# A recommendation tower on one core: packed dot products in two units per tile, eight one-hot features, gathers in two bursts

## The reference

```python
e = jnp.stack([tbl_0[ids[:, 0]], ..., tbl_25[ids[:, 25]]], axis=1)
combined = jnp.concatenate([dense_features[:, None, :], e], axis=1)    # 2048 x 27 x 128
interactions = jnp.einsum('bnd,bmd->bnm', combined, combined)
z = jnp.concatenate([dense_features, interactions[:, _TRIU_I, _TRIU_J]], axis=1)
h = jnp.concatenate([z, dense_features], axis=1)                       # 2048 x 607
h = jnp.maximum(h @ W_top1 + b_top1, 0.0)                              # 512 columns
h = jnp.maximum(h @ W_top2 + b_top2, 0.0)                              # 256 columns
y = h @ W_top3
```

## Time and profile before

| | |
|---|---|
| median of 3 runs | 604.8 us (597.53 to 605.89) |
| profiled execution | 598.93 us, span 597.2 us |
| mean granted clock of TensorE | 0.842 |
| TensorE busy | 466.2 us (78%), 6057 matmuls |
| VectorE, ScalarE, GpSimd busy | 256.7 us (43%), 176.1 us (29%), 296.0 us (50%) |

### The profile page before, as it was taken

How to read it: one execution, slowest core, us unless ns; L and a number is a source line. 1 busy time by engine, 2 the same in 40 slices (tenths; PEclk the granted TensorE clock), 3 DMA queues, 4 the chain that set the end, 5 groups by cost and what they waited for, 6 DMA issues and landing times.

```text
span 597.2 us, 14574 instructions
## 1 busy us (share of the span) xinstructions
PE 466.2 (78%) x6057; PEld 423.9 (71%) x6057; DVE 256.7 (43%) x465; ACT 176.1 (29%) x443; POOL 296.0 (50%) x314
## 2 busy tenths in 40 slices
PE   3564677697988889676997979688797969977787
PEld 1463666586977878576886868677686858877776
DVE  3853458251544446252452626344262623622340
ACT  1231233332324332132322314132232423224341
POOL 7777144554554455455554545555554554545200
PEclk9557689897878988888888979869797796988899
DMA  5453211111111111111111111111111111111000
GB/s 116 157 171 88 73 27 39 38 44 37 36 45 35 42 37 46 38 38 42 36 46 33 46 33 44 38 35 42 41 45 37 33 45 32 41 37 38 23 3 1
DMA packets 19577, 28.02 MB, mean 47 GB/s; under 512 B 10691, under 2 KB 13267, under 8 KB 19518
## 3 DMA queue, kind: packets, MB, share of 16 engines
q0 software_dynamic: 9728, 19.94, 12.7%
q1 hardware_dynamic: 9790, 7.17, 4.1%
HBM read 27.08 MB, written 0.01 MB: 45 GB/s over the span
## 4 chain that ended last, share of the span: by engine, by line
PE 71%; issue 15%; ACT 3%; DMA 3%; another core or an unknown queue 3%; DVE 3%; SPq 1%; DVEq 0%; ACTq 0%
PE dots_ps L394 27%; PE fetch_ps L419 22%; PE h_ps L466 9%; PE vec_ps L372 6%; PE h_ps L482 4%; DMA vecs<-in_tbl 3%; PE ids_ps L401 2%; ACT vecs L607 1%; PE fetch_ps L466 1%; DVE onehot L739 1%; ACT inter L643 1%; DVE inter L818 1%; DVE vecs L590 1%; ACT vecs L590 0%
## 5 line engine op out<-in xcount | busy, mean ns | idle before, releaser
L333 POOL DMA_INDIRECT rows<-in_tbl,idx x304 | 293.5, 965 | 262.5 <-DMA rows<-in_tbl,idx 154.4
L394 PE MATMUL dots_ps<-vecs 128*27 128x27 f32 x4096 | 162.3, 202 | 73.1 <-issue 71.6
L394 PEld LDWEIGHTS dots_ps<-vecs 128*27 128x27 f32 x4096 | 148.1, 118 | 88.4 <-issue 85.8
L419 PE MATMUL fetch_ps<-onehot,t_hi 125*128 125x256 f32 x448 | 136.0, 327 | 38.4 <-ACT vecs L607 24.7
L818 DVE COPY_PREDICATED inter<-mask,dots_ps 27x128 f32<-27x128 int32 (+2 forms) x256 | 66.7, 260 | 205.4 <-ACT inter L643 198.9
L739 DVE TENSOR_TENSOR onehot<-ids_ps,row_of 125x1024 fp32r<-125x1024 f32 x94 | 111.2, 1220 | 59.5 <-PE ids_ps L401 32.6
L419 PE MATMUL fetch_ps<-onehot,t_lo 125*128 125x256 f32 x448 | 133.5, 326 | 0.0
L419 PEld LDWEIGHTS fetch_ps<-onehot,t_hi 125*128 125x128 f32 x448 | 99.6, 222 | 43.0 <-issue 36.6
L643 ACT COPY inter<-dots_ps 27x128 f32<-27x128 f32 (+1 forms) x256 | 63.8, 249 | 179.9 <-PE dots_ps L394 106.1
L419 PEld LDWEIGHTS fetch_ps<-onehot,t_lo 125*128 125x128 f32 x448 | 100.0, 223 | 4.5 <-issue 0.2
L607 ACT COPY vecs<-fetch_ps 128x256 f32<-128x256 f32 x56 | 37.6, 672 | 125.8 <-PE fetch_ps L419 99.4
(11 more groups left out here) (65 smaller groups left out, 194.5 us busy)
## 6 DMA issues: line engine op xcount, KB each, us to landing
rows<-in_tbl,idx POOLq DMA_INDIRECT x304
vecs<-in_tbl SPq DMA_DIRECT2D x6, 500.0 KB
rows<-in_r_dense_features SPq DMA_DIRECT2D x16, 64.0 KB
h_sb<-in_W_top_laid SPq DMA_DIRECT2D x2, 512.0 KB
w_sb<-in_W_top SPq DMA_DIRECT2D x1, 512.0 KB
w_sb<-in_tbl SPq DMA_DIRECT2D x1, 500.0 KB
idx<-in_ids SPq DMA_DIRECT2D x16, 13.0 KB
w_dense<-in_W_top SPq DMA_DIRECT2D x1, 256.0 KB
```

What stands on the lines that cost most here:

```text
L333: nc.gpsimd.indirect_dma_start(out=rows[v % 2][:, s, :], out_offset=None, in_=tables[f - 1][:, :], in_offset=bass.IndirectOffsetOnAxis(ap= ...
L394: last = pe.matmul(dots_ps[q * 32:q * 32 + N, n // HALF, o:o + N], vs[:, b, :], vs[:, b, :], start=True, stop=True)
L419: last = pe.matmul(fetch_ps[:, 0:R], part[0:KP, k, h * KH + t, :], onehot[buf][h][0:KP, t, :], start=(h == 0 and t == 0 and part is t_hi), ...
```

## The change

It changes these things together.

1. *Dot products in pairs and units.* `vecs` gets 32 slots a sample instead of 27 (the last five zero). A matmul takes two samples: 64 stationary columns and 2 x 27 moving ones, of which the blocks of each sample with itself are used. A tile is two units of 32 such matmuls; `dots_ps` (two banks) holds one unit, so unit 1 waits until unit 0 is copied and merged. Half a unit ends with one `dots_done`.
2. *Out of PSUM.* Copies and merges are made for each unit: twice as many, of half the size. The dense rows are copied to `inter` ahead of the first.
3. *Gathers.* 18 features are gathered; a tile's gathers go in two bursts without waits inside: groups 0 and 1 (7 gathers) after unit 0 of tile v - 2, groups 2 to 4 (11) after its unit 1. In round 0's first tiles each group waits for the group before it. The program's DMA scratch size is given as 2048.
4. *Fetches.* Feature 1 is the eighth in `SPREAD`. `ids_ps`, `fetch_ps` and the layers' `mlp_ps` are single banks of 256 columns. A spread sits behind the first matmul of the second half of a fetch, or in the second half of a unit of dot products; the order of a step is new on every engine.
5. *Layers.* Layer 1 goes in four runs of 15 matmuls into two banks in turn, layer 2 in two runs of 8, between fetches and units; layer 3 gives y as a row of 256 columns, so it isn't transposed at the end.
6. *Start.* The ids of the eight features come laid out in rows, so nothing is transposed for them; each table comes in two DMAs, of 112 and 13 partitions, the ninth and further loads in another order; the spread, comparison and fetch of the first round go item by item.

```diff
-SPREAD = (5, 6, 9, 14, 18, 24, 26)
-
+SPREAD = (1, 5, 6, 9, 14, 18, 24, 26)
...
     Q = 4
-    QS = P // Q
-
+    UNITS = 2
+    QS = P // (UNITS * Q)
     COLS = 15
...
-    HALF = QS // 2
-    NA, ND = Q * Q + 1, Q * Q
-
+    PER_UNIT = Q * Q
+    NA, ND = UNITS * PER_UNIT + 1, UNITS * PER_UNIT
+    U = UNITS * 2
+
+
+    NP = 32
+    PAIR = 2 * N
+    SLOT = 64
+    assert QS * SLOT == 2 * 512 and PAIR <= SLOT
...
-        vecs = [sb(f"vecs{s}", [P, 2, P, N]) for s in range(2)]
-
...
-        dots_ps = ps("dots_ps", [P, 2, 512])
-        h1_ps = ps("h1_ps", [P, M1 // 2, R])
-        h2_ps = ps("h2_ps", [P, M2, R])
-        ids_ps = ps("ids_ps", [P, 512])
-        fetch_ps = ps("fetch_ps", [P, 512])
+        dots_ps = ps("dots_ps", [P, QS, SLOT])
+        ids_ps = ps("ids_ps", [P, 512])[:, 0:R]
+        fetch_ps = ps("fetch_ps", [P, 512])[:, 0:R]
+        mlp_ps = [ps(f"mlp_ps{m}", [P, 512])[:, 0:R] for m in range(2)]
...
+            def load_table(n):
+
+                src = tables[SPREAD[n] - 1].rearrange("(p t) d -> p (t d)", t=KT)
+                for a, b in ((0, 112), (112, KP)):
+                    sp.dma_start(staged_piece(n)[a:b], src[a:b]).then_inc(staged[n], 16)
...
-            def gather_tile(i, v, paced):
-
+            def gather_tile(i, v, first):
                 pool.wait_ge(idx_in[v], i * 16 + 16)
                 for k, group in enumerate(groups):
-
+                    mine = [s for s in group if ORDER[s]]
                     if k == 0:
+
                         pool.wait_ge(transposed, i * (4 * NG) + groups_of(v - 1))
-                    elif paced and k < 3:
-                        pool.wait_ge(dots_done, i * (4 * Q) + (v - 2) * Q + (0, 1, 4)[k])
-                    elif paced:
-                        pool.wait_ge(transposed, i * (4 * NG) + groups_of(v - 1) + (1, 4)[k - 3])
+                    if k == NG - 2 and first and v == 1:
+
+                        pool.wait_ge(dense_w_sum, 1)
+                    if first and v == 1:
+
+                        vv, kk = (v, k - 1) if k else (v - 1, NG - 1)
+                        n = len([s for s in groups[kk] if ORDER[s]])
+                        pool.wait_ge(gathered[vv % 2][kk], i * (32 * n) + (vv // 2 + 1) * 16 * n)
+                    elif k in (0, 2) and not (first and v < 2):
+
+                        pool.wait_ge(dots_done, i * (8 * UNITS) + (v - 2) * 2 * UNITS + (k // 2 + 1) * 2)
                     pool.sem_inc(groups_begun, 1)
-                    mine = [ORDER[s] for s in group if ORDER[s]]
-                    landed = i * (32 * len(mine)) + v // 2 * (16 * len(mine))
-                    for n, f in enumerate(mine):
-                        s = ORDER.index(f)
-                        if paced and n and n % AT_ONCE == 0:
-                            pool.wait_ge(gathered[v % 2][k], landed + 16 * n)
-                            pool.sem_inc(gathers_resumed, 1)
+                    for s in mine:
+                        f = ORDER[s]
                         nc.gpsimd.indirect_dma_start(
                             out=rows[v % 2][:, s, :], out_offset=None, in_=tables[f - 1][:, :],
                             in_offset=bass.IndirectOffsetOnAxis(ap=idx[v][:, f - 1:f].bitcast(U32), axis=0),
                         ).then_inc(gathered[v % 2][k], 16)
 
+            pool.memset(pick_f[:], 0.0).then_inc(picks_zero, 1)
+            pool.wait_ge(picks_zero, 1)
+            pool.affine_select(out=pick_f[:], in_=pick_f[:], compare_op=ALU.not_equal, fill=1.0, base=0,
+                               pattern=[[-1, X], [0, P]], channel_multiplier=1).then_inc(picks_made, 1)
             pool.iota(row_of_i[:], pattern=[[1, KT]], base=0, channel_multiplier=KT).then_inc(rows_counted, 1)
             pool.iota(mask_i[:], pattern=[[-1, JG]], base=0, channel_multiplier=1).then_inc(mask_begun, 1)
...
-            def dots(i, v):
+            def dots(i, v, u, spread=None):
-                for b in range(P):
-                    q, n = b // QS, b % QS
-                    o = (n % HALF) * N
-                    last = pe.matmul(dots_ps[q * 32:q * 32 + N, n // HALF, o:o + N], vs[:, b, :],
-                                     vs[:, b, :], start=True, stop=True)
-                    if n == QS - 1:
-                        last.then_inc(dots_done, 1)
+                if not (first and u == 0):
+
+                    pe.wait_ge(inter_by_act, i * (4 * NA) + v * NA + u * (1 + PER_UNIT))
+                    pe.wait_ge(inter_by_dve, i * (4 * ND) + v * ND + u * PER_UNIT)
+                for h in range(2):
+                    if h and spread:
+
+                        round_, k, m = spread
+                        pe.wait_ge(compared, m * 2)
+                    for n in range(QS):
+                        b = u * UNITS * 2 * QS + h * 2 * QS + n * 2
+                        last = pe.matmul(dots_ps[h * 64:h * 64 + 64, n, 0:PAIR],
+                                         vs[:, b:b + 2, :].rearrange("p b f -> p (b f)"), vs[:, b:b + 2, 0:N],
+                                         start=True, stop=True)
+                        if h and spread and n == 0:
+                            spread_ids(round_, k)
+                    last.then_inc(dots_done, 1)
...
-                        pe.wait_ge(compared, m * 2 + 2)
+                    if h == 0:
+                        if not (static(m) and m == 0):
+
+                            pe.wait_ge(fetched, m)
+                    elif spread:
+
+                        pe.wait_ge(compared, spread[2] * 2)
-                            if spreads and t == 0 and part is t_hi:
-                                spread_ids(for_round, k + 1)
+                            if spread and h == 1 and t == 0 and part is t_hi:
+                                spread_ids(*spread[:2])
                     last.then_inc(onehot_used, 1)
+            def fetch_item(i, r, k):
+                spread = {0: 1, 1: 3, 3: 4, 4: 6, 6: 8}
+                fetch(k, *item(i, r, k), spread_of(i, r, spread[k]) if k in spread else None)
...
-                    spread_ids(i * 2 + r + 1, 0)
-                    transpose_rows(i, v, after=with_layer1)
-                    fetch_items(i, r, BEFORE_DOTS)
-                    dots(i, v)
-                    layer1(*prev, 1)
-                    fetch_items(i, r, AFTER_LAYER1)
-                    transpose_rows(i, v + 1, after=with_layer2)
-                    fetch_items(i, r, AFTER_LAYER2)
-                    layer3(*prev)
-                    fetch_items(i, r, AFTER_LAYER3)
+                    transpose_rows(i, v, (0, 1))
+                    fetch_item(i, r, 0)
+                    transpose_rows(i, v, (2, 3, 4))
+                    layer1(*prev, 0)
                 else:
                     for k in range(X):
-                        spread_ids(0, k, k)
-                    fetch_first(range(EARLY))
...
-                dots(i, v + 1)
-                fetch_items(i, r, LAST if prev else [X - 2, X - 1])
+                        pe.wait_ge(lo_made, k + 1)
+                        if k == X - 1:
+                            pe.wait_ge(ids_cast, 2)
+                        fetch(k, k, k % 2, ((k + 1) // X, (k + 1) % X, k + 1))
...
+                    fetch_item(i, r, 0)
+                dots(i, v, 0, spread_of(i, r, 2))
+                fetch_item(i, r, 1)
+                if prev:
+                    layer1(*prev, 1)
+                    layer1(*prev, 2)
+                else:
+                    transpose_rows(i, v + 1, (0, 1))
+                fetch_item(i, r, 2)
+                dots(i, v, 1)
+                if prev:
+                    transpose_rows(i, v + 1, (0, 1))
+                    layer1(*prev, 3)
+                transpose_rows(i, v + 1, (2, 3, 4))
+                fetch_item(i, r, 3)
+                dots(i, v + 1, 0, spread_of(i, r, 5))
+                fetch_item(i, r, 4)
+                if prev:
+                    layer2(*prev, 0)
+                fetch_item(i, r, 5)
+                dots(i, v + 1, 1, spread_of(i, r, 7))
+                fetch_item(i, r, 6)
+                if prev:
+                    layer2(*prev, 1)
+                fetch_item(i, r, 7)
+                if prev:
+                    layer3(*prev)
...
+            def take_products(i, v, u):
+                if u == 0:
+                    if not (static(i) and i == 0 and v == 0):
+                        act.wait_ge(x_lo_made, i * 4 + v)
+                    nc.scalar.copy(inter[:, JG, :].rearrange("p (h two s) -> p h two s", two=2, s=QS),
+                                   in_turn(vecs[v // 2][:, v % 2, :, 0])).then_inc(inter_by_act, 1)
                 for q in range(Q):
-
-                    act.wait_ge(dots_done, i * (4 * Q) + v * Q + q + 1)
+                    act.wait_ge(dots_done, i * (8 * UNITS) + v * 2 * UNITS + u * 2 + q // 2 + 1)
                     for g in range(Q):
-                        nc.scalar.copy(inter_of(q, g, 0, count[g]),
```

(75 more changed lines are left out.)

538 lines of the change are left out of this document (217 added, 321 removed).

## The result

The changed kernel takes 692.3 us (median of 4, 690.69 to 694.52) where the kernel before takes 601.2: a ratio of 1.161 (1.154 to 1.167). Forecast were 580 us and a range of 540 to 640. But this ratio belongs to the chip on which it was measured: run again unaltered on three other chips, the same pair gave 674.4 for 595.8 us on chip 7, and 499.0 for 582.3 (ratio 0.859, 0.845 to 0.874) on chip 8 and 503.0 for 583.0 (0.866, 0.851 to 0.881) on chip 1. Both results have to be explained, and the two chips with a gain are what made it possible. Medians in this document are of all runs, while ratios leave out runs that were over 1.5% above the fastest of their kernel, which on chip 7 leaves one run of the changed kernel, 666.8 us.

The account below looks back on a forecast made before the run. TensorE was taken as the bound: 44.9 us of load a step plus 24.4 from gathers. Start 64, first step 60, six steps of 67 and tail 47 gave 573, or 580 us on the median's scale; range 540 to 640.

Parts of the forecast that it names:

- the price of a gather: TensorE's loss per gather in a loop step: 1.07 us beside dot products, 0.33 us beside other work.
- 0.33 is the near end: Gathers in long runs: at least 0.33 us each, since data and count stay the same; 27 such gathers cost 8.9 us.
- 24.4 us of a step are gathers' doing: Loop step before the change: TensorE's load 44.9 us, the other 24.4 us of 69.3 due to gathers.
- 45 us of a step and late for nobody: GpSimd after the change: busy 45 us a step, with rows wanted only a tile later.
- The dearest place: Third unit of dot products in each step: five gathers lie over it, so it takes some 8 us.
- Rival (a): Long gather runs hold TensorE up: 8 us per run of eleven, 1.5 for the other gathers; 631 us, chance 0.27.
- All else of a step: Loop step without gathers' cost: TensorE's work 45.6 us, plus 3 us of waits from VectorE's order.
- the 573: Sum over the whole span, in us: start 64, first step 60, six steps of 67, tail 47.
- The start: Before the first unit: comparisons set the pace, first fetch at about 14 us, eighth 41 later, unit 1 at 64.
- The merges' cover: Between units: fetches and layers of 6.1 to 13.9 us hide the 2.5 us wait for merges, so it costs nothing.
- (b): Chain of fetch, spread, comparison, fetch: half of eight links late by 1 us, a step 71 us, 599 in all; chance 0.15.
- (c): Dot products run clean past the gather runs: 57.5 us a step, 512 us, or 518 on the median's scale; chance 0.10.

Follow-up runs that it names:

- two bursts alone: Kernel before with a tile's gathers in two runs of 7 and 12 and no waits inside; 434.5 us on chip 1, 709.8 on chip 10.
- unpacked kernel: Changed kernel with one matmul for each sample again, all else as changed; 649.3 us on chip 10, ratio 1.086 to the kernel before.

## Why the prediction was wrong

Two steps failed, one for each kind of chip. Where the change was first measured, at 692 us, it was the price of a gather, "0.33 is the near end" in a long run and 1.07 beside dot products. On the chips without the stall it was the bound: "24.4 us of a step are gathers' doing", which I took for stalls of TensorE alone.

**The bound.** The rows were there: the earlier trace rows show the 2.3 us of landing wait ahead of a run of four, and 38 gathers at 1.8 us are 69 us, the step of 69.3. On the first chip two limits lay close together, TensorE stretched by stalls and GpSimd stretched by its own waits. TensorE waited for no gathered row there, and GpSimd had some 32 us to spare in the whole span, as its waits in the kernel before show:

```profile
POOL rows L333 <- DMA rows<-in_tbl,idx: 154.4, 64, 4.0
...
POOL rows L333 <- PE dots_ps L394: 31.7, 10, 9.4
```

I took all 24.4 us above TensorE's load for stalls, while on chips without them (1 and 8) the kernel before was only 14 to 20 us faster in all. Removing the pacing was worth 147 us there (582 to 435) and was priced at nothing. What the prediction said of GpSimd after the change, 45 us of a step and late for nobody, did hold on chip 1: GpSimd stood 67 us for dot products, and TensorE waited for no row.

**The price of a gather.** I took 1.07 us beside dot products and 0.33 elsewhere, 18.5 us a step. A step of the changed kernel is 82.9 us with the stall and 55.0 without (330.2 us for six on chip 1): 27.9 us, 0.77 a gather. On a free chip it is nothing. The dearest place is the one that was named, the third unit of a step, but at 12.6 to 14.1 us from its first start to its last instead of some 8, while first units, with no gather beside them, take 3.9. Rival (a) had the mechanism: it said 8 us of hold for each run of eleven, and the signals in the run above came 7 to 9 us late. Its sign came as well: ScalarE stood 166 us, in 22 waits, for fetches without a releaser in the profile. It had been given a chance of 0.27. It said 631 us where 690.8 were measured, because it rested on the same sum for all else.

**All else of a step.** 45.6 + 3 = 48.6 was forecast and 55.0 measured on chip 1. The dot products take 16.2 us for 12.3, three units of 4.16 us with a spread inside and one of 3.75 without. An instruction of the packed dot products takes 58.5 ns (34 in 1.99 us, 64 in 3.75), not 48, so 256 are 15.0 us, and the spreads, which the sum had with the fetches, are the other 1.2. Packing thus lost 1.1 us a step to the 13.9 of 512 single instructions.
The Trainium skill's rule (TensorE: Matmul & The Clock Gate, LDWEIGHTS), that the load takes columns / 1.2 ns, was weighed in the prediction and not taken; by it 53 ns for 64 columns, an estimate, and the measurement lies nearer to that than to my 48.
The eight fetches take 18.8 us in the first loop step for 17.6: a fetch with a spread takes 2.4 us to the next work's start and one without 2.0 to 2.2, where the sum took 2.2 and left out one of the 16 matmuls (the earlier trace rows have 15 in 2.00 us). TensorE's waits were 3.6 us a step for my 3. The last 0.7 us fits the clock: three of the six steps take 53.9 us at a granted 1.00, two take 58.2 and 58.5 at 0.94.

**The pieces.** With the stall: start 67.9 for 64, first step 73.8 for 60, six steps 497 for 402, tail 52.0 for 47, in all 118 us above the 573. On chip 1: 64.3, 54.7, 330.2 and 52.7. The start was right in mechanism and size where nothing stalls (first fetch at 13.1 us for 14, the eighth 42.9 later for 41), but not as a gain: on chip 1 the kernel before begins its first unit at 53.1 us, 11 earlier. VectorE's load was right too (37 us a step for 38). The merges' cover held: TensorE waited for them 0.7 us in all on chip 1. The tail was 5 us too low on both.

**The smaller scratch.** It cost nothing measurable on a free chip, where the changed kernel with and without gathers took the same time. The changed kernel was not run with the default size, nor the kernel before with 2048 bytes on a chip that stalls, and whether the size alters a held signal stays open.

**Rivals (b) and (c).** (b) was not seen: fetches waited for comparisons 3.8 us in all on chip 1. (c), clean dot products, is what chips 1 and 8 do: 518 forecast, 499 and 503 measured, the stall's absence and not a shift in time being the reason.

**What is open.** Why one chip holds TensorE's signals beside gathers and another doesn't no run tells. That it is the chip and not its history isn't separated either.

On the free chips the change's gain is all in the pacing: two bursts alone give 434.5 and the whole change 503.0. The other 68 us are the loop's 55.0 for 47.7 (44 in six steps), start 10, first step 4 and tail 10.

## What to carry to other kernels

Before pricing anything against an engine that is half idle, multiply its own issue period, waits included, by the count in a step: where that is the length of the step, it is a bound, even if another engine's stalls fill the same time. A version with one kind of work left out says in one look what that work costs; here the gathers of one program cost 0 us on chip 8, and by the same 434.7 us without them 275 on chip 10, where it takes 709.8. And where a forecast hangs on stalls that no instruction explains, run both kernels on several chips before believing a sign: here the change went from 14% faster to 16% slower.

## What the runs showed of the hardware

A chip can hold TensorE's completion signals up to 9 us while indirect gathers are in flight, and let a few of its instructions pass each 0.7 us, and another chip with the same program does neither. With two bursts, the 256 instructions of a tile's dot products took 6.97 us on chips 1 and 8, and 14.2 to 17.3 on chip 10, each time with gathers beside them (6.97 in the last tile, with none).

Single matmuls went at nearly twice the pace where they alternate between two groups of 32 output partitions. In the unpacked kernel's tail, a unit alone:

```profile
600.51 1.87 PE L332 MATMUL dots_ps<-vecs 128*27 128x27 f32 x128
```

128 instructions in 1.87 us are 14.6 ns each, for 27.1 in the kernel before, where 32 samples in a row go to the same partitions; their starts come in pairs 5 to 7 ns apart. I had not expected that. The unpacked kernel also has its vectors in 32 slots instead of 27, and no run tells the two apart; that the alternation does it is my reading. It may be why the unpacked form was no slower with the stall (649 us; the packed one took 674 and 692 on other chips that stall), which no run shows. The Trainium skill (TensorEngine Tiling (Array Packing), Key Properties) has it that different tiles can load weights and multiply in parallel, and the trace agrees. By an estimate, two bursts with alternating single matmuls would take some 6 us a step off TensorE's 47.7 (2 x 6.97 for 2 x 3.8), but hardly off the 434.5 us: 38 gathers at 1.25 us are 47.5 us a step, which would then be the bound. That wasn't run.
